# The close of the first routed MLP: norm factors in halves between other operations, five tiles on VectorE, beta added in the MLP

## The chip, the cores and the metric

The program runs on one core of one Trainium2 chip. The metric is its time on the device in microseconds. A core has TensorE (matrix products), VectorE (DVE in the profile), ScalarE (ACT), GpSimd (POOL) and SyncE (SP, here only a queue of DMA issues). Each engine works through its own list of instructions in order; engines meet by semaphores.

## The reference

The program is an audio tower of four layers. 32 sequences of 125 tokens are cut to 87 tokens each, 2784 tokens of width 192, and then pass attention and feed-forward blocks. The change lies in the feed-forward block of layer 0 and in how its result is made ready for layer 1:

```
def _L0_ffn_ref(x, w1, b1, w2, b2, down_w, down_b, up_w, gamma, beta):
    logits = _gelu(x @ w1 + b1) @ w2 + b2
    routing = softmax(logits); sparse = the two largest of 8, scaled to sum 1
    z = _gelu(einsum('bsh,ehd->bsed', x, down_w) + down_b)
    expert_out = einsum('bsed,edh->bseh', z, up_w)
    moe_out = einsum('bseh,bse->bsh', expert_out, sparse)
    return _layer_norm(x + moe_out, gamma, beta)

h = h + _L0_ffn_ref(_layernorm(h), ...)
h = h + _L1_attn_ref(_layernorm(h), ...)     # quantises its input by its largest absolute value
```

## The kernel before

Tokens lie in 22 tiles of 128 (the last has 96), `H` is the residual h and `X` (`l0f_x`) its normalised copy x, both [128, 22, 192] in SBUF. The program is a row of stages; each is a block in which every engine has its own list, and all engines meet at its end. `Kit.stage` also counts semaphores: once more than 100 have been given out, it clears them on GpSimd (L105) and adds a barrier of all engines (L106) ahead of the stage that is opened.

The stages around the change are l0f_router, l0f_dispatch, l0f_mlp (the routed MLP, 51 tiles of 128 routed rows), l0f_tail, l1a_turn, l1a_qkv and so on; l1a_close is stage 19 and l1f_front stage 20.

In l0f_mlp (`routed_mlp_stage`) GpSimd gathers the rows of a tile by an indirect DMA (L852), TensorE turns and expands them, ScalarE applies gelu (L963), TensorE projects, VectorE multiplies by the routing weight (L1005), and GpSimd scatters the result to DRAM (L856). The function has an argument `beside`: an operation that VectorE does behind the multiplication of each of the first 22 tiles. Two later MLPs use it, this one does not.

l0f_tail then closes the block. The tiles go in four parts (`PARTS`: 6, 6, 5 and 5 tiles). SyncE issues ten loads of the routed rows into `back` (L1940). VectorE adds beta to all of `H` (L1964), clears the unused rows of `back` (L1966), and then by parts adds both choices to `X` (L1970) and takes the statistics of each tile (L1972). `find_factors` (L1947 to L1962) makes from them the mean, the variance and 1/std of all 22 tiles at once: six steps, a square root on ScalarE (L2000), seven steps more. Each step is issued by `link`, which waits until the one before has ended. ScalarE applies the factors, one operation a tile (L2004), and reports each part. VectorE follows by parts: times gamma (L1976), plus `H` (L1977), which is the new residual, and its statistics (L1979). The same again for the norm of layer 1: factors of all 22 tiles, ScalarE applies them, VectorE takes the largest absolute value by parts (L1985) and over the parts (L1986), and GpSimd over the partitions (L1991).

The order of the work is the order of these lists; nothing else schedules it.

Of the kernel before, what the change touches and what calls it, by code (L numbers as in the profile page):

```python
# [16 lines left out]
ALU = mybir.AluOpType  # L17
ACT = mybir.ActivationFunctionType
# [11 lines left out]
D = 192  # L30
TP = 128
# [1797 lines left out]
def l0_ffn(kit, H, stats, X1, l1a):  # L1829
    nc, dram = kit.nc, kit.dram  # L1830
    E, R = 8, 96
    with ExitStack() as outer:
# [77 lines left out]
        routed_mlp_stage(kit, "l0f_mlp", route, ex, ACT.Gelu)  # L1910
# [3 lines left out]
PARTS = ((0, 6), (6, 12), (12, 17), (17, 22))  # L1914


def l0f_tail_stage(kit, route, X, H, gb, stats, x_max):
# [5 lines left out]
    R = route.choices  # L1923
    with kit.stage("l0f_tail") as ctx:
# [18 lines left out]
        def _(dve):  # L1943
            link, v = Chain(dve, chain), nc.vector

            def find_factors(u):
                dve.wait_ge(stats_done, (u + 1) * TN)  # L1947
                me, ve, mo, vo = (stats[:, :, k] for k in (1, 2, 4, 5))
                link(v.tensor_tensor(tmp[u][:], me, mo, ALU.subtract))
                link(v.scalar_tensor_tensor(mean[u][:], tmp[u][:], 0.5, mo, ALU.mult, ALU.add))  # L1950
                link(v.scalar_tensor_tensor(tmp[u][:], tmp[u][:], D / 4.0, tmp[u][:], ALU.mult, ALU.mult))
                link(v.tensor_tensor(var[u][:], vo, tmp[u][:], ALU.add))
                link(v.tensor_tensor(var[u][:], var[u][:], ve, ALU.add))
                v.tensor_scalar(var[u][:], var[u][:], 1.0 / D, LN_EPS, ALU.mult, ALU.add).then_inc(var_ready, 1)
# [12 lines left out]
            for q, (a, z) in enumerate(PARTS):  # L1967
# [5 lines left out]
            find_factors(0)  # L1973
            for q, (a, z) in enumerate(PARTS):
                dve.wait_ge(applied, q + 1)
                link(v.tensor_tensor(X[:, a:z, :], X[:, a:z, :], across(gb[:, 0, :], 1, z - a), ALU.mult))  # L1976
                link(v.tensor_tensor(H[:, a:z, :], X[:, a:z, :], H[:, a:z, :], ALU.add))  # L1977
# [1853 lines left out]
```

## Time and profile before

| | us |
|---|---|
| median of 3 runs | 2314.96 |
| lowest and highest run | 2313.03, 2317.95 |
| span of the profiled execution | 2358.7 |
| l0f_tail, first load issued to the last small reduction's start | 697.75 to 756.15 |
| TensorE busy | 1698.8 (72%) |
| VectorE busy | 1290.5 (55%) |
| ScalarE busy | 1022.7 (43%) |
| GpSimd busy | 343.4 (15%) |

The profiled execution's own time is not listed apart from its span, which is from its first instruction to its last. Durations below come from that one execution. Times in the timelines are from the start of its span. An instruction's own duration can overlap that of the next on the same engine; where a row stands for several (x22), its duration is the time that they cover together.

### The profile page before, as it was taken

Reading aid. Unit: us, or ns where it says so; the run is one execution under the profiler, and the core shown is the slowest. Engines: PE = TensorE matmul, PEld = TensorE weight load, DVE = VectorE, ACT = ScalarE, POOL = GpSimd, SP = SyncE. Lnnn points to the kernel's source line nnn. Section 1 sums busy time; section 2 is a strip of 40 time slices with the busy share of each in tenths; the row PEclk is TensorE's granted clock in tenths of the full one; section 3 lists DMA queues with packets and bytes.
Section 4 is the critical chain, followed back from the end, with each engine's and each line's share of the span. In section 5 each row is a group of like instructions: output and inputs, shape, how many; then the busy total and the mean of one; then the engine's idle time right before and its main releaser. Section 6 shows DMA issues by size and latency. Waiting matters only on the chain. (4 is left out here: it accounts for less than half of the span.)

```text
span 2358.7 us, 35978 instructions
## 1 busy us (share of the span) xinstructions
PE 1698.8 (72%) x12150; PEld 1375.5 (58%) x12166; DVE 1290.5 (55%) x2688; ACT 1022.7 (43%) x2115; POOL 343.4 (15%) x415
## 2 busy tenths in 40 slices
PE   3588879856760489966499686664893698469995
PEld 2265657745650355545489563443683598369995
DVE  6588963361137879968622468997316211642223
ACT  4466753312234568865112147873322254312221
POOL 0000000006640000001143100000000342034431
PEclk9799979977885589986699797775996699689998
DMA  3200000214450000000466300000004453446775
GB/s 85 71 18 19 21 23 9 49 50 128 136 164 16 2 7 7 5 1 12 140 214 212 108 4 8 7 4 1 13 1 127 135 179 118 130 139 223 223 218 191
DMA packets 137245, 189.82 MB, mean 80 GB/s; under 512 B 51661, under 2 KB 111213, under 8 KB 137069
## 3 DMA queue, kind: packets, MB, share of 16 engines
q1 hardware_dynamic: 116289, 146.91, 20.3%
q0 software_dynamic: 15360, 36.72, 5.4%
q10 hardware_dynamic: 5420, 3.91, 0.6%
q8 instruction: 103, 1.69, 0.3%
q14 instruction: 73, 0.60, 0.1%
HBM read 150.21 MB, written 33.68 MB: 78 GB/s over the span
## 5 line engine op out<-in xcount | busy, mean ns | idle before, releaser
L989 DVE TENSOR_TENSOR 36_l3f_mlp_hidden<-36_l3f_mlp_gate,36_l3f_mlp_first 128x512 f32<-128x512 f32 x51 | 35.1, 688 | 185.0 <-ACT 36_l3f_mlp_gate L967 101.0
L882 PE MATMUL 36_l3f_mlp_first<-36_l3f_mlp_xT,36_l3f_mlp_w 128*128 128x128 f32 x816 | 101.5, 278 | 1.8 <-issue 1.8
L1245 PE MATMUL 2_performer_p_u<-perf_proj,2_performer_yT 128*87 128x512 f32 (+1 forms) x204 | 94.1, 605 | 10.6 <-DVE 2_performer_arg L1406 9.5
L882 PEld LDWEIGHTS 36_l3f_mlp_first<-36_l3f_mlp_xT,36_l3f_mlp_w 128*128 128x128 f32 x816 | 96.9, 195 | 2.1 <-issue 2.1
L1005 DVE TENSOR_SCALAR 9_l0f_mlp_y<-9_l0f_mlp_second,l0f_routing_weight 128x192 f32<-128x192 f32 x51 | 20.4, 416 | 142.0 <-PE 9_l0f_mlp_second L896 64.4
L967 ACT ACTIVATE 36_l3f_mlp_gate<-36_l3f_mlp_first 128x512 f32<-128x512 f32 x51 | 30.5, 597 | 136.4 <-PE 36_l3f_mlp_first L887 127.4
L1003 DVE TENSOR_TENSOR 32_l3a_mlp_y<-32_l3a_mlp_second,l3a_experts_b_rows 128x192 f32<-128x192 f32 x29 | 10.4, 358 | 136.7 <-issue 106.3
L896 PE MATMUL 36_l3f_mlp_second<-l3f_experts_w,36_l3f_mlp_hidden 128*128 x408 | 81.0, 342 | 0.0
L989 DVE TENSOR_TENSOR 22_l1f_mlp_hidden<-22_l1f_mlp_gate,22_l1f_mlp_first 128x512 f32<-128x512 f32 x29 | 19.9, 687 | 105.8 <-ACT 22_l1f_mlp_gate L967 78.2
L963 ACT ACTIVATE 32_l3a_mlp_hidden<-32_l3a_mlp_first,l3a_experts_b_cols 128x128 f32<-128x128 f32 x174 | 48.1, 377 | 65.5 <-PE 32_l3a_mlp_first L887 47.6
L2618 ACT ACTIVATE l1a_p<-14_pla_f,l1a_recip 128x87 int16<-128x87 f32 x272 | 71.7, 354 | 9.2 <-DVE l1a_recip L2693 9.2
L856 POOL DMA_INDIRECT l3f_results<-36_l3f_mlp_y,l3f_routing_put x51 | 50.2, 984 | 136.2 <-DVE 36_l3f_mlp_y L1005 136.2
L896 PEld LDWEIGHTS 36_l3f_mlp_second<-l3f_experts_w,36_l3f_mlp_hidden 128*128 128x128 f32 x408 | 66.0, 192 | 6.5 <-issue 0.5
L1245 PEld LDWEIGHTS 2_performer_p_u<-perf_proj,2_performer_yT 128*87 128x87 f32 x204 | 33.3, 177 | 60.2 <-issue 57.6
L896 PE MATMUL 32_l3a_mlp_second<-l3a_experts_w,32_l3a_mlp_hidden 128*128 x348 | 66.0, 341 | 2.6 <-ACT 32_l3a_mlp_hidden L963 2.6
L896 PE MATMUL 9_l0f_mlp_second<-l0f_experts_w,9_l0f_mlp_hidden 128*128 x204 | 53.5, 391 | 19.7 <-issue 15.9
L963 ACT ACTIVATE 9_l0f_mlp_hidden<-9_l0f_mlp_first,l0f_experts_b_cols 128x128 f32<-128x128 f32 x102 | 32.0, 363 | 71.9 <-PE 9_l0f_mlp_first L887 44.8
L930 ACT ACT_TABLE_LOAD x4 | 5.1, 1283 | 133.4 <-PEq L605 92.9
L896 PEld LDWEIGHTS 32_l3a_mlp_second<-l3a_experts_w,32_l3a_mlp_hidden 128*128 128x128 f32 x348 | 57.4, 194 | 6.9 <-issue 3.7
L887 PE MATMUL 36_l3f_mlp_first<-36_l3f_mlp_xT,36_l3f_mlp_w 64*128 64x128 f32 x816 | 60.2, 286 | 0.5 <-issue 0.3
L882 PE MATMUL 22_l1f_mlp_first<-22_l1f_mlp_xT,22_l1f_mlp_w 128*128 128x128 f32 x464 | 58.6, 280 | 1.0 <-issue 0.9
L1879 POOL PARTITION_ALL_REDUCE l1a_mx<-6_l0f_hidden_wide x1 | 0.4, 387 | 404.5 <-issue 404.5
(914 smaller groups left out, 4964.0 us busy)
## 6 DMA issues: line engine op xcount, KB each, us to landing
36_l3f_mlp_w<-in_L_ffn_w_dram SPq DMA_DIRECT2D x51, 768.0 KB
22_l1f_mlp_w<-in_L_ffn_w_dram SPq DMA_DIRECT2D x29, 768.0 KB
32_l3a_mlp_w<-in_L_attn_W_dram SPq DMA_DIRECT2D x29, 576.0 KB
9_l0f_mlp_w<-in_L_ffn_down_w_dram SPq DMA_DIRECT2D x51, 192.0 KB
l3a_experts_w<-in_L_attn_W_dram SPq DMA_DIRECT2D x8, 576.0 KB
l1a_blocks<-l1a_qkb SPq DMA_DIRECT2D x192, 5.4 KB, 1.8
l1f_experts_w<-in_L_ffn_w_dram SPq DMA_DIRECT2D x8, 384.0 KB, 6.1
l2a_blocks<-l2a_qkb SPq DMA_DIRECT2D x192, 5.4 KB, 1.8
```

The costliest lines, as they stand in the source:

```text
L856: nc.gpsimd.indirect_dma_start(route.results, to(i), y[i % NY][:], None).then_inc(put[i % NY], 16)
L882: nc.tensor.matmul(to(t + a * PAIRS), of[:, t + a * PAIRS, :], at[:, 0, :], start=(t == 0), stop=True, skip_group_check=True)
L887: ins = nc.tensor.matmul(to(t + a * PAIRS), of[rows, 2 * PAIRS + t, :], at[rows, 1, :], start=False, stop=True, skip_group_check=True)
L896: ins = nc.tensor.matmul(second[j % 2][:, 0:D], hidden[j % 2][:, t, :], ex.w2[:, ds(expert[j], 1), t, :].rearrange("p a w -> p (a w)"), st ...
L930: nc.scalar.preload_act_table(func)
L963: ins = nc.scalar.activation(out[:, t], src[:, t // PAIRS, t % PAIRS, :], func, bias=ex.b1_cols[:, ds(e, 1), t])
L967: nc.scalar.activation(out[:], src[:, 0, 0:HT, :], func).then_inc(done, 1)
L989: v.tensor_tensor(hidden[j % 2][:], gate[j % 2][:], first[j % 2][1][:, 0, 0:HT, :], ALU.mult).then_inc(hidden_done, 1)
L1003: ins = v.tensor_tensor(y[i % NY][:], of, ex.b2_rows[:, ds(e, 1), :].rearrange("p a w -> p (a w)"), ALU.add)
L1005: ins = v.tensor_scalar(y[i % NY][:], of, route.weight[:, i:i + 1], None, ALU.mult)
L1245: ins = t.matmul(p_u[:, k, 0:(EIGHT - h) * M], yT[b % 2][:, k, :], proj[:, h:EIGHT, :].rearrange("p h m -> p (h m)"), start=True, stop=True)
L2618: ins = a(P[:, j, n, :], f[j % 2][:, n * NT:(n + 1) * NT], ACT.Copy, scale=recip[:, j, n:n + 1])
```

## The change

1. Beta goes into the routed MLP: 22 additions of 128 x 192, by `beside` (L1911 of the new kernel), in place of one of 128 x 4224 in the tail. The clearing of `back` goes to GpSimd.
2. The factors are made by halves (`HALF`: tiles 0 to 11 and 12 to 21). `find_factors` becomes a generator: each `next` issues one step, and the next step waits for it before it is issued. The steps of one half stand between the sums, products and statistics of the other half's parts; only the second half's factors of the second norm (and six steps of those of the first) stand in a row.
3. The last part of the second norm, five tiles, is applied by VectorE with `tensor_scalar`, and its maximum is taken first.
4. Three semaphores are added (`factor`, `cleared`, `summed`). With them the clearing in `Kit.stage` falls ahead of l1a_close, before it fell ahead of l1f_front; and one of the later clearings has five ranges where it had four.

```diff
-        routed_mlp_stage(kit, "l0f_mlp", route, ex, ACT.Gelu)
+        routed_mlp_stage(kit, "l0f_mlp", route, ex, ACT.Gelu,
+                         beside=lambda link, v, i: link(v.tensor_tensor(H[:, i, :], H[:, i, :], gb[:, 1, :], ALU.add)))
...
+HALF = ((0, 2), (2, 4))
...
-                link(v.tensor_tensor(tmp[u][:], me, mo, ALU.subtract))
-                link(v.scalar_tensor_tensor(mean[u][:], tmp[u][:], 0.5, mo, ALU.mult, ALU.add))
...
-            link(v.tensor_tensor(H[:], H[:], across(gb[:, 1, :], 1, TN), ALU.add))
-            for r in range(R):
-                link(v.memset(back[r][LAST:TP, TN - 1, :], 0.0))
...
+            def find_factors(u, h):
+                a, z = span(h)
...
+                dve.wait_ge(stats_done, u * TN + z)
+                small(v.tensor_tensor(t, me, mo, ALU.subtract))
+                yield
+                wait_small()
+                small(v.scalar_tensor_tensor(m, t, 0.5, mo, ALU.mult, ALU.add))
+                yield
...
+                v.tensor_scalar(w, w, 1.0 / D, LN_EPS, ALU.mult, ALU.add).then_inc(var_ready, 1)
+                yield
+                dve.wait_ge(std_ready, 2 * u + h + 1)
+                small(v.reciprocal(r, s))
+                yield
...
+            def collect(q, steps):
+                a, z = PARTS[q]
                 dve.wait_ge(loaded[q], 16 * R * (2 if z == TN else 1))
                 for r in range(R):
-                    link(v.tensor_tensor(X[:, a:z, :], X[:, a:z, :], back[r][:, a:z, :], ALU.add))
+                    v.tensor_tensor(X[:, a:z, :], X[:, a:z, :], back[r][:, a:z, :], ALU.add).then_inc(summed, 1)
+                    done["summed"] += 1
+                    some(steps)
+                    dve.wait_ge(summed, done["summed"])
                 for i in range(a, z):
                     v.bn_stats(stats[:, i, :], X[:, i, :]).then_inc(stats_done, 1)
+                    some(steps)
...
+            none = iter(())
+            dve.wait_ge(cleared, R)
+            collect(0, none)
+            collect(1, none)
+            early = find_factors(0, 0)
+            collect(2, early)
+            collect(3, early)
+            whole(early)
+            late = find_factors(0, 1)
+            some(late, 6)
+            close(0, late)
+            whole(late)
+            close(1, none)
+            early = find_factors(1, 0)
+            some(early)
+            close(2, early)
+            close(3, early)
+            whole(early)
+            whole(find_factors(1, 1))
+            dve.wait_ge(factors_ready, 4)
+            a, z = PARTS[MINE]
+            for i in range(a, z):
+                v.tensor_scalar(X[:, i, :], H[:, i, :], rstd[1][:, i:i + 1], less[1][:, i:i + 1], ALU.mult,
+                                ALU.add).then_inc(summed, 1)
+            dve.wait_ge(summed, done["summed"] + z - a)
+            link(v.memset(X[LAST:TP, TN - 1, :], 0.0))
+            largest(MINE)
+            for q in range(MINE):
                 dve.wait_ge(applied, len(PARTS) + q + 1)
...
+            root(0, 0)
+            act.wait_ge(factors_ready, 1)
+            apply(0, 0, X)
+            root(0, 1)
+            apply(0, 1, X)
+            act.wait_ge(factors_ready, 2)
+            apply(0, 2, X)
+            apply(0, 3, X)
+            root(1, 0)
+            act.wait_ge(factors_ready, 3)
+            root(1, 1)
+            apply(1, 0, H)
+            apply(1, 1, H)
+            act.wait_ge(factors_ready, 4)
+            apply(1, 2, H)
```

`close` is `collect` for gamma and the residual: product, a step, sum, a step, and a step behind each tile's statistics. `some` issues one step (or n), `whole` all that are left.

On VectorE, from the sums of the third part on, the list before was this (`l0f_x` is `X`, `10_l0f_tail_back` the routed rows, x5 is five in a row):

```order
L1970 TENSOR_TENSOR l0f_x<-l0f_x,10_l0f_tail_back 128x960 x2
L1972 BN_STATS stats<-l0f_x 128x6 x5
L1970 TENSOR_TENSOR l0f_x<-l0f_x,10_l0f_tail_back 128x960 x2
L1972 BN_STATS stats<-l0f_x 128x6 x5
L1949 TENSOR_TENSOR 10_l0f_tail_tmp<-stats 128x22
L1950 SCALAR_TENSOR_TENSOR 10_l0f_tail_mean<-10_l0f_tail_tmp,stats 128x22
L1951 SCALAR_TENSOR_TENSOR 10_l0f_tail_tmp<-10_l0f_tail_tmp 128x22
L1952 TENSOR_TENSOR 10_l0f_tail_var<-stats,10_l0f_tail_tmp 128x22
L1953 TENSOR_TENSOR 10_l0f_tail_var<-10_l0f_tail_var,stats 128x22
```

and is now this, down to the fourth statistics of that part:

```order
L2014 TENSOR_TENSOR l0f_x<-l0f_x,10_l0f_tail_back 128x960
L1964 TENSOR_TENSOR 10_l0f_tail_tmp<-stats 128x12
L2014 TENSOR_TENSOR l0f_x<-l0f_x,10_l0f_tail_back 128x960
L1967 SCALAR_TENSOR_TENSOR 10_l0f_tail_mean<-10_l0f_tail_tmp,stats 128x12
L2019 BN_STATS stats<-l0f_x 128x6
L1970 SCALAR_TENSOR_TENSOR 10_l0f_tail_tmp<-10_l0f_tail_tmp 128x12
L2019 BN_STATS stats<-l0f_x 128x6
L1973 TENSOR_TENSOR 10_l0f_tail_var<-stats,10_l0f_tail_tmp 128x12
L2019 BN_STATS stats<-l0f_x 128x6
L1976 TENSOR_TENSOR 10_l0f_tail_var<-10_l0f_tail_var,stats 128x12
L2019 BN_STATS stats<-l0f_x 128x6
L1979 TENSOR_SCALAR 10_l0f_tail_var<-10_l0f_tail_var 128x12
```

The steps of the first half's factors have moved up from behind all statistics to behind each of the third and fourth part's operations.

On ScalarE the tail's list before was:

```order
L1997 ACT_TABLE_LOAD
L2000 ACTIVATE 10_l0f_tail_std<-10_l0f_tail_var 128x22
L2004 ACTIVATE l0f_x<-l0f_x,10_l0f_tail_less,10_l0f_tail_rstd 128x192 x22
L2000 ACTIVATE 10_l0f_tail_std<-10_l0f_tail_var 128x22
L2004 ACTIVATE l0f_x<-H,10_l0f_tail_less,10_l0f_tail_rstd 128x192 x22
```

and is now:

```order
L2084 ACT_TABLE_LOAD
L2089 ACTIVATE 10_l0f_tail_std<-10_l0f_tail_var 128x12
L2093 ACTIVATE l0f_x<-l0f_x,10_l0f_tail_less,10_l0f_tail_rstd 128x192 x6
L2089 ACTIVATE 10_l0f_tail_std<-10_l0f_tail_var 128x10
L2093 ACTIVATE l0f_x<-l0f_x,10_l0f_tail_less,10_l0f_tail_rstd 128x192 x16
L2089 ACTIVATE 10_l0f_tail_std<-10_l0f_tail_var 128x12
L2089 ACTIVATE 10_l0f_tail_std<-10_l0f_tail_var 128x10
L2093 ACTIVATE l0f_x<-H,10_l0f_tail_less,10_l0f_tail_rstd 128x192 x17
```

The root is taken four times for a half each, the second one between the first two parts, the last two together ahead of the second norm's tiles, of which ScalarE keeps 17.

## Rows read from the trace of the kernel before

**Rows 1.** Busy times by stretch of l0f_tail: length, busy us of each engine, PEclk.
```profile
core 0: us, PE busy (x) PEld busy (x) DVE busy (x) ACT busy (x) POOL busy (x), PEclk, DMA share, GB/s
...
719.30:725.30 6.00, 0.00 (x0) 0.00 (x0) 2.53 (x14) 3.00 (x8) 0.00 (x0) 0.50 0.00 0
...
741.50:747.50 6.00, 0.00 (x0) 0.00 (x0) 2.53 (x14) 3.00 (x8) 0.00 (x0) 0.50 0.00 0
```

**Rows 2.** Timeline of l0f_tail, first factors: start us, us, engine line op [idle before <-releaser].
```profile
717.87 1.40 DVE L1972 BATCH_NORM_STATS2 stats<-l0f_x 128x6 f32<-128x192 f32 x5
719.30 0.20 DVE L1949 TENSOR_TENSOR 10_l0f_tail_tmp<-stats 128x22 f32<-128x22 f32 x1
...
720.44 0.18 DVE L1954 TENSOR_SCALAR 10_l0f_tail_var<-10_l0f_tail_var 128x22 f32<-128x22 f32 x1
720.65 0.22 ACT L2000 ACTIVATE 10_l0f_tail_std<-10_l0f_tail_var 128x22 f32<-128x22 f32 x1 [21.61 <-DVE 10_l0f_tail_var L1954]
720.90 0.29 DVE L1956 RECIPROCAL 10_l0f_tail_rstd<-10_l0f_tail_std 128x22 f32<-128x22 f32 x1 [0.29 <-ACT 10_l0f_tail_std L2000]
...
722.52 9.75 ACT L2004 ACTIVATE l0f_x<-l0f_x,10_l0f_tail_less,10_l0f_tail_rstd 128x192 f32<-128x192 f32 x22 [1.65 <-DVE 10_l0f_tail_less L1962]
725.29 1.36 DVE L1976 TENSOR_TENSOR l0f_x<-l0f_x,l0f_gb 128x1152 f32<-128x1152 f32 x1 [2.80 <-ACT l0f_x L2004]
```

**Rows 3.** The same timeline, second factors and end of the stage.
```profile
741.49 0.20 DVE L1949 TENSOR_TENSOR 10_l0f_tail_tmp<-stats 128x22 f32<-128x22 f32 x1
...
744.72 9.74 ACT L2004 ACTIVATE l0f_x<-H,10_l0f_tail_less,10_l0f_tail_rstd 128x192 f32<-128x192 f32 x22 [1.66 <-DVE 10_l0f_tail_less L1962]
...
754.96 1.15 DVE L1985 TENSOR_REDUCE 10_l0f_tail_part_max<-l0f_x 128x1 f32<-128x960 f32 x1
756.15 0.16 DVE L1986 TENSOR_REDUCE 10_l0f_tail_row_max<-10_l0f_tail_part_max 128x1 f32<-128x4 f32 x1
```

**Rows 4.** The same timeline, start of the stage.
```profile
697.75 4.92 SPq L1940 DMA_DIRECT2D 10_l0f_tail_back<-l0f_results  x10
...
697.80 4.56 DVE L1964 TENSOR_TENSOR H<-H,l0f_gb 128x4224 f32<-128x4224 f32 x1 [3.18 <-PEq L806]
702.45 0.53 DVE L1966 MEMSET 10_l0f_tail_back<- 32x192 f32 x2
703.10 2.75 DVE L1970 TENSOR_TENSOR l0f_x<-l0f_x,10_l0f_tail_back 128x1152 f32<-128x1152 f32 x2
```

**Rows 5.** Timeline of l3f_out, the last stage, which issues the same loads.
```profile
2337.75 6.06 SPq L1070 DMA_DIRECT2D 37_l3f_out_back<-l3f_results  x10
2343.01 2.75 DVE L1090 TENSOR_TENSOR H<-H,37_l3f_out_back 128x1152 f32<-128x1152 f32 x2 [8.41 <-DMA 37_l3f_out_back<-l3f_results]
...
2346.90 5.14 DVE L1090 TENSOR_TENSOR H<-H,37_l3f_out_back 128x1152 f32<-128x1152 f32 x4 [1.14 <-DMA 37_l3f_out_back<-l3f_results]
```

**Rows 6.** Groups of the routed MLP (busy us, mean ns, idle us); another MLP's addition.
```profile
L856 POOL DMA_INDIRECT l0f_results<-9_l0f_mlp_y,l0f_routing_put x51 | 49.7, 974 | 46.3 <-DVE 9_l0f_mlp_y L1005 34.9 <-issue 11.3
...
L1005 DVE TENSOR_SCALAR 9_l0f_mlp_y<-9_l0f_mlp_second,l0f_routing_weight 128x192 f32<-128x192 f32 x51 | 20.4, 416 | 142.0 <-PE 9_l0f_mlp_second L896 64.4 <-remote 42.8 <-issue 34.8
...
L2266 DVE TENSOR_TENSOR H<-H,l3a_x x22: 348/349/350, 1873.5 to 1969.3; 128x192 f32<-128x192 f32 x22
```

**Rows 7.** Timeline of VectorE in an earlier stage, 12-wide operations, no wait between.
```profile
116.10 0.16 DVE L1435 TENSOR_TENSOR 2_performer_arg<-2_performer_rmax,2_performer_p_top 87x12 f32<-87x12 f32 x1 [5.31 <-PE 2_performer_p_top L1257]
116.19 0.22 DVE L1440 RECIPROCAL 2_performer_rden<-2_performer_p_out 87x12 f32<-87x12 f32 x1
```

**Rows 8.** Timeline of VectorE, 22 tiles normalised with two pointer operands.
```profile
458.84 6.46 DVE L211 TENSOR_SCALAR l0f_x<-H,5_norm_mean,5_norm_rstd 128x192 f32<-128x192 f32 x22
```

**Rows 9.** Gaps ahead of l1a_close and l1f_front; the clearing (ns min/median/max).
```profile
1086.12 0.06 DVE L3072 MEMSET 19_l1a_close_m<- 128x1 f32 x1 [0.60 <-PEq L2718]
...
1115.37 0.20 DVE L1767 TENSOR_TENSOR 20_l1f_front_tmp<-stats 128x22 f32<-128x22 f32 x1 [2.18 <-PEq L106]
...
L105 POOLq DRAIN  x19: 57/88/112, 532.8 to 2052.1; - x19
L105 POOLq EVENT_SEMAPHORE_RANGE_CLEAR  x19: 46/174/243, 532.9 to 2052.5; - x19
```

More of the change, by code:

```diff
@@ L1923, in l0f_tail_stage @@
     R = route.choices
+    MINE = len(PARTS) - 1
     with kit.stage("l0f_tail") as ctx:
@@ L1968, in _, with some, whole @@
+            def some(steps, n=1):
+                for _ in range(n):
+                    next(steps, None)
+            def whole(steps):
+                for _ in steps:
+                    pass
+            def collect(q, steps):
+                a, z = PARTS[q]
                 dve.wait_ge(loaded[q], 16 * R * (2 if z == TN else 1))
                 for r in range(R):
-                    link(v.tensor_tensor(X[:, a:z, :], X[:, a:z, :], back[r][:, a:z, :], ALU.add))
+                    v.tensor_tensor(X[:, a:z, :], X[:, a:z, :], back[r][:, a:z, :], ALU.add).then_inc(summed, 1)
+                    done["summed"] += 1
+                    some(steps)
+                    dve.wait_ge(summed, done["summed"])
@@ L1971, in _, with close @@
                 for i in range(a, z):
                     v.bn_stats(stats[:, i, :], X[:, i, :]).then_inc(stats_done, 1)
-            find_factors(0)
-            for q, (a, z) in enumerate(PARTS):
+                    some(steps)
+            def close(q, steps):
+                a, z = PARTS[q]
                 dve.wait_ge(applied, q + 1)
-                link(v.tensor_tensor(X[:, a:z, :], X[:, a:z, :], across(gb[:, 0, :], 1, z - a), ALU.mult))
-                link(v.tensor_tensor(H[:, a:z, :], X[:, a:z, :], H[:, a:z, :], ALU.add))
+                v.tensor_tensor(X[:, a:z, :], X[:, a:z, :], across(gb[:, 0, :], 1, z - a), ALU.mult).then_inc(summed, 1)
+                done["summed"] += 1
+                some(steps)
+                dve.wait_ge(summed, done["summed"])
+                v.tensor_tensor(H[:, a:z, :], X[:, a:z, :], H[:, a:z, :], ALU.add).then_inc(summed, 1)
+                done["summed"] += 1
+                some(steps)
+                dve.wait_ge(summed, done["summed"])
@@ L1978, in _, with largest @@
                 for i in range(a, z):
                     v.bn_stats(stats[:, i, :], H[:, i, :]).then_inc(stats_done, 1)
-            find_factors(1)
-            for q, (a, z) in enumerate(PARTS):
+                    some(steps)
+            def largest(q):
+                a, z = PARTS[q]
+                link(v.tensor_reduce(part_max[:, q:q + 1], X[:, a:z, :], AX.XY, ALU.max, apply_absolute_value=True))
+            none = iter(())
+            dve.wait_ge(cleared, R)
+            collect(0, none)
@@ L1989, in _ @@
         def _(pool):
+            for r in range(R):
+                nc.gpsimd.memset(back[r][LAST:TP, TN - 1, :], 0.0).then_inc(cleared, 1)
             pool.wait_ge(maxed, 1)
@@ L1997, in _, with root, apply @@
             nc.scalar.preload_act_table(ACT.Sqrt)
[L1998 to L2005 removed]
+            def root(u, h):
+                a, z = span(h)
+                act.wait_ge(var_ready, 2 * u + h + 1)
+                a_(std[u][:, a:z], var[u][:, a:z], ACT.Sqrt).then_inc(std_ready, 1)
+            def apply(u, q, of):
+                for i in range(*PARTS[q]):
+                    ins = a_(X[:, i, :], of[:, i, :], ACT.Identity, bias=less[u][:, i:i + 1], scale=rstd[u][:, i:i + 1])
+                ins.then_inc(applied, 1)
+            root(0, 0)
[13 more added lines that the diff above has]
+            apply(1, 2, H)
 def l1_ffn(kit, H, stats, l2a, l2a_arrived, l2a_loads):
```

70 lines of the change are left out of this document (40 added, 30 removed).

## The prediction

> **What bounds the kernel now.** I read the page first: one core, TensorE the busiest engine over the whole span, so a gain on VectorE counts only where TensorE has nothing to do. I then took the busy times by stretches of the stage that is changed (l0f_tail), the timeline of that stage, the timelines of two other stages for prices, and the groups of the routed MLP ahead of it.
>
> The stage has no TensorE work, and its end sets when the next stage can start. Its path is: loads of the routed rows, VectorE's sums and statistics, 13 small steps for the norm factors, ScalarE's first six tiles, VectorE again, the small steps again, ScalarE again, VectorE's maxima. In the two stretches around the factors VectorE is busy 2.53 of 6.00 us [rows 1]: there the small steps run one by one, and then VectorE waits 2.80 us for ScalarE's first part [rows 2, 3]. The clock column says 0.50 there, so TensorE is at 1.2 GHz before and will be at 1.2 GHz after: it is idle either way.
>
> **Beta (part 1).** The 4.56 us addition and the two memsets (0.53 us) stand ahead of the first sum, which starts at 703.10, 5.35 us after the first load was issued [rows 4]. The last stage of the kernel issues the same loads (two blocks of 128 x 1152 first) with nothing on VectorE ahead, and its first sum starts 2343.01 - 2337.75 = 5.26 us after the issue [rows 5]. So the addition lies almost wholly in the shadow of the loads: with it gone the first sum starts at about 697.75 + 5.26 = 703.0, at best 0.1 us earlier. I take 0.05. What is late next is the load itself. The second part's rows land 9.15 us after the issue by [rows 5], 706.90; VectorE wants them at 707.4, so they stay hidden, by 0.5 us. The memsets go to GpSimd, idle there; they would have to take over 5 us to be seen.
>
> In the routed MLP the addition comes back as 22 pieces of 128 x 192. The same piece in another routed MLP takes 349 ns; with its wait some 0.39 us. VectorE is idle 142 us before its 51 multiplications there, 2.8 us a tile [rows 6], so I take 0. If every piece delayed its tile it would be 22 x 0.39 = 8.6 us; that end is kept.
>
> **Interleaved small steps (part 2).** A step that waits for the one before costs 0.23 us (719.30 to 720.44 for five) [rows 2]. One with no such wait costs less: a 12-wide operation on VectorE starts at 116.10 and the next at 116.19 [rows 7], so 0.09 us at most; I take 0.085. Behind a sum or a product, whose result is waited for anyway, I take 0.025 (0 to 0.05). The reciprocal (290 ns against 180) I take at 0.2. It also needs ScalarE's root: from the last variance step to the reciprocal pass 0.46 us [rows 2], while one statistics operation (0.26, from five in 1.40) and the step itself give 0.35, so a stall of 0.1.
>
> On this the Trainium skill speaks against the change: "VectorE: DVE Perf Modes", section "The DRAIN you can't avoid", says that the next operation does not start until the pipe is empty, with or without semaphores between, and its rules for authors say to reduce the number of operations and not of semaphores. The rows disagree: 0.09 us from start to start [rows 7], while the first operation itself is shown with 0.16 us. By that rule the interleaving would win nothing; it is a rival below.
>
> Now the path, on the clock of the profiled execution:
> - First half's factors. They are hidden in parts 2 and 3 of the collecting. Part 2 grows by 4 x 0.085 + 0.2 + 0.1 + 2 x 0.025 = 0.69, part 3 by 3 x 0.085 = 0.26 up to the place of the last step. This stands ahead of the fifth statistics operation, before at 717.87 + 4 x 0.264 = 718.93; now 718.93 - 0.05 + 0.95 = 719.83. ScalarE starts 0.21 us later, as it did after the last step [rows 2], at 720.04. Before: 722.52. Gain so far 2.5 us, and VectorE's product of part 0 starts at 725.29 - 2.48 = 722.81. In the meantime VectorE finishes collecting (720.3) and does six waited steps of the second half (1.3 us, 721.6): not late.
> - The products, sums and statistics took 725.29 to 741.49, 16.20 us [rows 2, 3]. They take up the rest: part 0 gets seven steps, the reciprocal under a product (5 x 0.085 + 0.05 = 0.48); ahead of part 2 there is one step with a wait for the last statistics (0.2); part 2 gets seven (0.69); part 3 gets five, two of them under a product or a sum (0.31). Sum 1.68, so 722.81 + 17.88 = 740.69. The gain has shrunk to 0.8 us: the interleaving pays back its own steps, since VectorE is full here. ScalarE's parts 1 to 3 keep ahead: part 1 is done at some 725.7, and is wanted at 727.6.
> - Last factors. Only the second half's 13 steps are left in a row. ScalarE no longer waits for them: it waits for the first half (ready) and for the second half's variance, which is six steps in: 740.69 + 1.1 + 0.21 = 742.0, then the root, and its first tile at 742.14. Before: 744.72 [rows 3]. A gain of 2.6 us.
> - Five tiles to VectorE. ScalarE has 17 tiles instead of 22, at 9.75 us for 22 (0.439 each and 0.1 more): done at 742.14 + 7.56 = 749.70. VectorE: factors at 740.69 + 3.2 = 743.9, five tiles at 6.46/22 = 0.29 each [rows 8], 745.4, memset 0.25, maximum of its own part 1.19 (754.96 to 756.15, [rows 3]), 746.9, part 0 to 748.3, part 1 to 749.7. So both engines come to the last maximum together at 749.7, and the small reduction starts at 750.9. Before: 756.15. The stage gains 5.25 us.
>
> **Elsewhere (part 3).** The stage allocates three more semaphores. The helper that clears them once over 100 are used now does so one stage earlier, ahead of l1a_close and no longer ahead of l1f_front. The gap on VectorE is 0.60 us without and 2.18 us with the clearing [rows 9], so some 1.6 us move and nothing is gained: both are barriers of all engines. One further clear is issued later on (20 against 19), a drain and a range clear of 0.09 + 0.17 us [rows 9]: 0.26 us lost.
>
> **Sum.** 5.25 - 0.26 = 5.0 us. The profiled execution has a span of 2358.7 us, so it would come to 2353.7. The runs have 2314.96 as their median, 43.7 us less than that span; the stage has no TensorE work whose clock could explain a part of this, so I carry the 5.0 us over unscaled: 2314.96 - 5.0 = 2310.0 us. A measurement of this kernel can tell about 0.2% (4.6 us) from no change, so the forecast lies right at that bound.
>
> **Rivals.**
> 1. Full price for every small step. If a step behind another operation costs 0.22 instead of 0.085, 22 of them on the path take 22 x 0.135 = 3.0 us back: gain 2.0, 2313.0 us. For it: the rule cited above, and that each step still has a wait instruction ahead of it. Against it: [rows 7].
> 2. Beta really comes off the path. If the loads land soon after 698, the whole 4.56 + 0.53 us goes too, as the diff suggests at first sight: 2310.0 - 5.0 = 2305.0 us. Against it: the 5.26 us with an idle VectorE [rows 5].
> 3. Slower: beta delays the routed MLP. Each piece sits in VectorE's queue ahead of the next tile's multiplication, for which GpSimd's scatter and, two tiles on, TensorE wait. Price up to 0.39 us a piece, 8.6 us, giving 2318.6 us. It decides from 5.0/22 = 0.23 us exposed per piece on: then the kernel is slower than before. For it: of 46.3 us that GpSimd idles ahead of its scatters, 34.9 are put down to VectorE's product. Against it: 2.8 us of idle VectorE a tile [rows 6].
> 4. The clearing, moved, or what comes after the shorter stage, costs or gives a few us in the TensorE stages behind. Nothing in the rows asks for it.
>
> **How the numbers follow.** Forecast 0.62, rival 1 0.12, rival 2 0.06, rival 3 0.10, the rest 0.10. The forecast's own range is 2308 to 2312: small steps wholly hidden would give 1.9 us more, 0.05 us more per step 1.1 us less. The three runs of the kernel before lie between 2313.0 and 2318.0, so about 2 us of spread comes on either side, and rival 1 and a part of rival 3 lie inside: 2305.5 to 2315.5. Faster by over 0.2% (below 2310.3): six tenths of the forecast, rival 2, a third of the rest: 0.47. Slower by over 0.2% needs nearly all of rival 3 or something unseen: 0.09. Within: 0.44.
>
> **What would show it.** The first sum at 5.2 to 5.4 us after the first load issue (step 1; 1 us or less would be rival 2). VectorE start to start of a small step between two statistics 0.08 to 0.09 us (0.22: rival 1). ScalarE's first tile of the first pass some 22.3 us after the issue, of the second some 44.4 us; the last maximum some 52 us after it, with VectorE waiting less than 0.5 us there. The routed MLP as long as before, to 1 us. The gap ahead of l1a_close 1.6 us longer and that ahead of l1f_front 1.6 us shorter. The prediction is wrong if the stage gains under 4 or over 6 us, or if the MLP or a stage behind moves by over 2 us.

## The result and the profile after

The changed kernel took 2310.57 us (median of 20 runs, 2304.79 to 2317.28) against 2315.53 us for the kernel before (20 runs on the same chip, 2311.29 to 2337.33). The ratio is 0.9968 [0.9954, 0.9981], so 4.4 to 10.7 us faster. Measured twice more it was 0.9975 [0.9956, 0.9993] and 0.9973 [0.9954, 0.9992].

The profiled execution of the changed kernel has a span of 2307.4 us. In it the changed stage goes from its first load (669.03) to the start of the small reduction (721.92) in 52.89 us. Before it took 756.15 - 697.75 = 58.40 us [rows 3, 4]. The stage gained 5.51 us; 5.25 were forecast. All times "after the issue" below are counted from that first load, since the stage now starts earlier in the span.

The start of the stage in the timeline of the changed kernel (start, duration, engine line operation, idle time before), which answers to [rows 4]:

```profile
669.03 5.32 SPq L1944 DMA_DIRECT2D 10_l0f_tail_back<-l0f_results  x10
...
674.56 2.75 DVE L2014 TENSOR_TENSOR l0f_x<-l0f_x,10_l0f_tail_back 128x1152 f32<-128x1152 f32 x2 [8.69 <-DMA 10_l0f_tail_back<-l0f_results]
677.35 1.66 DVE L2019 BATCH_NORM_STATS2 stats<-l0f_x 128x6 f32<-128x192 f32 x6
```

With nothing on VectorE ahead of it the first sum still starts only 5.53 us after the issue, and it is the DMA that ends the wait. The two memsets now lie on GpSimd and are over at 669.48.

The same timeline from the last statistics of the collecting to the product of part 0, which answers to [rows 2]:

```profile
691.13 0.15 DVE L2000 SCALAR_TENSOR_TENSOR 10_l0f_tail_less<-10_l0f_tail_mean,10_l0f_tail_rstd 128x12 f32<-128x12 f32 x1
...
691.33 2.73 ACT L2093 ACTIVATE l0f_x<-l0f_x,10_l0f_tail_less,10_l0f_tail_rstd 128x192 f32<-128x192 f32 x6 [3.98 <-DVE 10_l0f_tail_less L2000]
691.59 0.18 DVE L1964 TENSOR_TENSOR 10_l0f_tail_tmp<-stats 128x10 f32<-128x10 f32 x1
...
692.63 0.17 DVE L1979 TENSOR_SCALAR 10_l0f_tail_var<-10_l0f_tail_var 128x10 f32<-128x10 f32 x1
693.97 0.19 ACT L2089 ACTIVATE 10_l0f_tail_std<-10_l0f_tail_var 128x10 f32<-128x10 f32 x1
...
694.09 1.36 DVE L2025 TENSOR_TENSOR l0f_x<-l0f_x,l0f_gb 128x1152 f32<-128x1152 f32 x1 [1.28 <-ACT l0f_x L2093]
```

ScalarE's first tile comes at 691.33, 22.30 us after the issue; before it was 722.52 - 697.75 = 24.77. What VectorE does meanwhile are six waited steps of the second half (each of them waits for the end of the one before), 0.21 us apart. It then waits 1.28 us for ScalarE's six tiles, where it waited 2.80 us.

The same timeline, second factors and end, which answers to [rows 3]:

```profile
711.66 0.18 DVE L1964 TENSOR_TENSOR 10_l0f_tail_tmp<-stats 128x10 f32<-128x10 f32 x1
...
712.70 0.17 DVE L1979 TENSOR_SCALAR 10_l0f_tail_var<-10_l0f_tail_var 128x10 f32<-128x10 f32 x1
712.98 0.21 ACT L2089 ACTIVATE 10_l0f_tail_std<-10_l0f_tail_var 128x10 f32<-128x10 f32 x1 [5.83 <-DVE 10_l0f_tail_var L1979]
713.09 7.54 ACT L2093 ACTIVATE l0f_x<-H,10_l0f_tail_less,10_l0f_tail_rstd 128x192 f32<-128x192 f32 x17
...
714.70 1.54 DVE L2063 TENSOR_SCALAR l0f_x<-H,10_l0f_tail_rstd,10_l0f_tail_less 128x192 f32<-128x192 f32 x5
...
716.59 3.93 DVE L2039 TENSOR_REDUCE 10_l0f_tail_part_max<-l0f_x 128x1 f32<-128x960 f32 x3
720.73 1.15 DVE L2039 TENSOR_REDUCE 10_l0f_tail_part_max<-l0f_x 128x1 f32<-128x960 f32 x1 [0.21 <-ACT l0f_x L2093]
721.92 0.16 DVE L2071 TENSOR_REDUCE 10_l0f_tail_row_max<-10_l0f_tail_part_max 128x1 f32<-128x4 f32 x1
```

ScalarE starts its second pass 0.39 us after the sixth step of the second half, and does not wait for the other seven. It does 17 tiles; VectorE does its own five at 0.30 us each and then the maxima. The last maximum waits 0.21 us for ScalarE: both engines arrive together.

Busy times by stretch around the two sets of factors, answering to [rows 1] (length, PE, PEld, DVE, ACT, POOL busy, PEclk):

```profile
690.60:696.60 6.00, 0.00 (x0) 0.00 (x0) 4.51 (x15) 5.28 (x13) 0.00 (x0) 0.50 0.00 0
711.70:717.70 6.00, 0.00 (x0) 0.00 (x0) 5.11 (x20) 4.72 (x12) 0.00 (x0) 0.50 0.00 0
```

VectorE is busy 4.51 and 5.11 us of 6, where it was 2.53, and ScalarE 5.28 and 4.72 where it was 3.00. The granted clock stays 0.50, that is 1.2 GHz, with TensorE idle, as before.

The interleaved steps themselves, from the last part of the collecting (690.12 to 690.79) and from the third and fourth part of the second pass (706.75 on; VectorE, five pieces of one timeline):

```profile
690.12 0.16 DVE L1991 TENSOR_SCALAR 10_l0f_tail_tmp<-10_l0f_tail_tmp 128x12 f32<-128x12 f32 x1
690.18 0.35 DVE L2019 BATCH_NORM_STATS2 stats<-l0f_x 128x6 f32<-128x192 f32 x1
690.45 0.15 DVE L1994 TENSOR_TENSOR 10_l0f_tail_tmp<-10_l0f_tail_tmp,10_l0f_tail_rstd 128x12 f32<-128x12 f32 x1
...
690.79 0.15 DVE L1997 TENSOR_TENSOR 10_l0f_tail_rstd<-10_l0f_tail_rstd,10_l0f_tail_tmp 128x12 f32<-128x12 f32 x1
...
706.75 0.15 DVE L1979 TENSOR_SCALAR 10_l0f_tail_var<-10_l0f_tail_var 128x12 f32<-128x12 f32 x1
706.82 0.35 DVE L2034 BATCH_NORM_STATS2 stats<-H 128x6 f32<-128x192 f32 x1
...
707.18 0.23 DVE L1982 RECIPROCAL 10_l0f_tail_rstd<-10_l0f_tail_std 128x12 f32<-128x12 f32 x1
...
707.54 0.15 DVE L1985 TENSOR_TENSOR 10_l0f_tail_tmp<-10_l0f_tail_rstd 128x12 f32<-128x12 f32 x1
707.61 1.15 DVE L2025 TENSOR_TENSOR l0f_x<-l0f_x,l0f_gb 128x960 f32<-128x960 f32 x1
708.67 0.17 DVE L1988 TENSOR_TENSOR 10_l0f_tail_tmp<-10_l0f_tail_tmp,10_l0f_tail_var 128x12 f32<-128x12 f32 x1
708.79 1.16 DVE L2029 TENSOR_TENSOR H<-l0f_x,H 128x960 f32<-128x960 f32 x1
```

A step whose result the next operation does not need starts 0.06 to 0.07 us ahead of that operation (707.54 to 707.61), though it is itself shown with 0.15 us. From one step to the next, with a statistics operation of 0.27 us between (690.12, 690.45 and 690.79), it is 0.33 to 0.34 us, so 0.07 for the step. Between two of the 960-wide operations a step costs nothing: they start 1.18 us apart with one (707.61, 708.79), and 1.18 us apart without one in the kernel with the steps in a row (below: 709.27, 710.45).

The routed MLP, groups of the changed kernel that answer to [rows 6], with beta's 22 pieces (busy us, mean ns | idle us ahead):

```profile
L1005 DVE TENSOR_SCALAR 9_l0f_mlp_y<-9_l0f_mlp_second,l0f_routing_weight 128x192 f32<-128x192 f32 x51 | 21.3, 418 | 107.3 <-DMA l0f_results<-9_l0f_mlp_y,l0f_routing_put 78.0 <-PE 9_l0f_mlp_second L896 29.2
...
L1911 DVE TENSOR_TENSOR H<-H,l0f_gb 128x192 f32<-128x192 f32 x22 | 7.7, 349 | 0.0
```

Beta takes 7.7 us of VectorE, and VectorE still idles 107.3 us ahead of its 51 multiplications.

The clearing, answering to [rows 9]:

```profile
1052.36 0.06 DVE L3177 MEMSET 19_l1a_close_m<- 128x1 f32 x1 [2.12 <-PEq L106]
...
1080.02 0.20 DVE L1767 TENSOR_TENSOR 20_l1f_front_tmp<-stats 128x22 f32<-128x22 f32 x1 [0.58 <-PEq L3093]
```

```profile
L105 POOLq DRAIN  x20: 54/78/107, 532.0 to 2007.0; - x20
L105 POOLq EVENT_SEMAPHORE_RANGE_CLEAR  x20: 68/133/243, 532.1 to 2007.1; - x20
```

The gap ahead of l1a_close is 2.12 us (0.60 before) and that ahead of l1f_front 0.58 us (2.18 before). One clear more is issued, 20 and not 19; what it costs on the way to the end no row shows.

### The profile page after: what moved, and what is told of

It reads as the page before. It is cut to its first block and busy times, and to the rows that moved or that the text cites. A ratio compares the mean times of both kernels' runs of the same rounds, so it can differ in the third digit from the quotient of the medians.

```text
span 2307.4 us, 36049 instructions
## 1 busy us (share of the span) xinstructions
PE 1687.5 (73%) x12166; PEld 1356.6 (59%) x12166; DVE 1299.0 (56%) x2738; ACT 1023.1 (44%) x2112; POOL 345.4 (15%) x417
## 5 line engine op out<-in xcount | busy, mean ns | idle before, releaser
L1005 DVE TENSOR_SCALAR 9_l0f_mlp_y<-9_l0f_mlp_second,l0f_routing_weight 128x192 f32<-128x192 f32 x51 | 21.3, 418 | 107.3 <-DMA l0f_results<-9_l0f_mlp_y,l0f_routing_put 78.0
L949 ACT ACTIVATE 36_l3f_mlp_xT<-36_l3f_mlp_turned,36_l3f_mlp_nw 128x128 f32<-128x128 f32 x102 | 31.9, 364 | 65.7 <-PE 36_l3f_mlp_turned L869 51.1
L896 PE MATMUL 9_l0f_mlp_second<-l0f_experts_w,9_l0f_mlp_hidden 128*128 x204 | 48.0, 359 | 15.2 <-DVE 9_l0f_mlp_y L1005 8.2
```

Source lines behind the costliest of these rows:

```text
L896: ins = nc.tensor.matmul(second[j % 2][:, 0:D], hidden[j % 2][:, t, :], ex.w2[:, ds(expert[j], 1), t, :].rearrange("p a w -> p (a w)"), st ...
L949: ins = nc.scalar.activation(xT[j % 2][:, k], turned[j % 2][:, k, 0:ROWS], ACT.Identity, scale=nw[j % NW][:, k:k + 1])
L1005: ins = v.tensor_scalar(y[i % NY][:], of, route.weight[:, i:i + 1], None, ALU.mult)
```

## The experiments

Each kernel was timed against the kernel before, on the same chip as those sent with it. "Stage" is from the first load's issue to the start of the small reduction, in the profiled execution. The first sum starts 5.3 to 5.7 us after the issue, as the loads land. Counted from the sum of the second part's rows, which leaves that out, the stage takes 48.7 us in both executions of the kernel before (707.46 to 756.15 in the first) and 43.0 us in all three of the changed kernel; where it matters, this count is given too.

**The changed kernel again.** No edit.

> The changed kernel once more, beside the kernel before. The closing stage took 58.4 us (first load issued to small reduction) before and 52.9 after, 5.5 us less; if the gain is there alone, the time is 5 to 5.5 us below the kernel before (ratio 0.9978). If the routed MLP ahead of it has become shorter too (it was 28 us shorter in the profile), the ratio is clearly lower, towards 0.988, and the MLP in this profile again takes some 139 us from the end of the dispatch to the first load of the closing stage, not 167.

Measured: 2311.25 us, ratio 0.9975 [0.9956, 0.9993]; stage 52.8 us, first sum 5.5 us after the issue. The stage's length repeats to 0.1 us. What follows: differences of a few tenths of a us in the stage can be read from single profiles, while the whole time can't show them.

**The kernel before again**, for its profile.

> The kernel before once more, one profile. If the length of the first routed MLP (167 us in the first profile of before, 139 in that of the changed kernel) is a matter of the execution and not of the change, it may come near 139 here too, with a span near 2312. If the additions of beta make the MLP faster, it stays at 167.

Measured: 2313.55 us (one run), span 2311.3 us; stage 58.3 us, first sum 5.27 us after the issue. Here the clearest difference is in the routed MLP. Windows over the MLP up to the first load, of the execution that the prediction was made from, of this one and of the changed kernel's:

```profile
531.00:698.00 167.00, 123.69 (x714) 99.11 (x714) 21.68 (x58) 50.47 (x155) 99.17 (x102) 0.85 0.45 131
```

```profile
529.00:667.00 138.00, 109.15 (x715) 86.45 (x714) 22.95 (x59) 50.44 (x155) 99.22 (x102) 0.94 0.54 159
```

```profile
530.00:669.00 139.00, 110.06 (x714) 87.38 (x714) 28.40 (x80) 50.30 (x154) 100.08 (x102) 0.94 0.54 158
```

TensorE is busy 109.15 us in 138.0 us here and 110.06 in 139.0 us in the changed kernel, both at a clock of 0.94. In the execution that the prediction was made from the same stretch took 167.2 us at 0.85, with TensorE busy 123.69 us and the DMA engines 0.45 of the time against 0.54; why it took longer no run shows. So the 51 us between that span and the changed kernel's are no effect of the change: the kernel before, profiled again, has 47.4 us less itself, 29.6 of them in this MLP. Its stage is the same to 0.1 us.

**Beta back in the tail**, the rest changed.

```
-routed_mlp_stage(kit, "l0f_mlp", route, ex, ACT.Gelu, beside=...)
+routed_mlp_stage(kit, "l0f_mlp", route, ex, ACT.Gelu)
...
+            link(v.tensor_tensor(H[:], H[:], across(gb[:, 1, :], 1, TN), ALU.add))
             collect(0, none)
```

> The changed kernel with beta again added in one piece at the head of the closing stage. Shadow theory: the 4.56 us addition lies beside the loads, the first sum starts 5.3 to 5.6 us after the first load's issue as without it, the closing stage takes 52.9 us to 0.2, the time is that of the changed kernel to 0.1%. Rival (the move is worth its 4.6 us): the first sum starts some 9.9 us after the issue or the stage is 4 us longer.

Measured: 2309.14 us, ratio 0.9980 [0.9956, 1.0003], stage 52.7 us. The start of its stage in the timeline:

```profile
664.82 5.12 SPq L1943 DMA_DIRECT2D 10_l0f_tail_back<-l0f_results  x10
...
664.87 4.56 DVE L2041 TENSOR_TENSOR H<-H,l0f_gb 128x4224 f32<-128x4224 f32 x1 [3.18 <-PEq L806]
670.14 2.75 DVE L2013 TENSOR_TENSOR l0f_x<-l0f_x,10_l0f_tail_back 128x1152 f32<-128x1152 f32 x2 [0.71 <-DMA 10_l0f_tail_back<-l0f_results]
```

The addition of 4.56 us is back on VectorE, and yet the first sum starts 5.32 us after the issue, and it has waited 0.71 us for the DMA by then. Moving beta is worth nothing in this stage.

**Beta in the MLP alone**: the kernel before, with the 22 pieces in the MLP and without the addition in the tail (the reverse of the diff above, on the kernel before).

> The kernel before with only beta moved into the routed MLP (the clearing of the two buffers stays on VectorE). Shadow theory: same as before, closing stage 58.4 us to 0.3, ratio 1.000. If the 22 pieces cost anything in the MLP: up to 0.39 us each, 8.6 us, ratio up to 1.0037. If the move is worth the addition: ratio 0.998, closing stage 54 us.

Measured: 2315.92 us, ratio 1.0001 [0.9969, 1.0033]; the MLP 138.4 us up to the first load, against 137.6 and 139.2 us in the executions above; stage 58.3 us. It brings nothing in the tail. In the MLP the 8.6 us are ruled out, but a small cost is not. From the end of the dispatch to the first load, the nine profiles with the pieces show 138.1 to 139.6 us (mean 138.8). Two without them show 137.6 (the kernel before) and 138.3 (beta back in the tail); the first profile, with its 167.2 us, is left out. So a cost of up to 1 us or so is neither shown nor excluded.

**Steps in a row.** The halves stay, but each half's steps are issued together instead of one by one behind other operations.

```
-                    some(steps)
...
-            early = find_factors(0, 0)
-            collect(2, early)
-            collect(3, early)
-            whole(early)
+            whole(find_factors(0, 0))
+            collect(2, none)
+            collect(3, none)
...
-            close(0, late)
+            close(0, none)
...
-            early = find_factors(1, 0)
-            some(early)
-            close(2, early)
-            close(3, early)
-            whole(early)
+            whole(find_factors(1, 0))
+            close(2, none)
+            close(3, none)
```

> The changed kernel with each half's small steps in a row where they begin, none between other operations. Cheap-between theory (a step between two others costs some 0.075 us, in a row 0.21): VectorE has 3.2 us for the first half's factors ahead of the third part, 1.6 us behind part 0 and 3.2 us ahead of part 2 of the second pass, and the closing stage comes to some 57.5 us (52.9 in the changed kernel), the time to that of the kernel before within 1 us. Rival (the pipe empties behind each operation in any case, so that interleaving wins nothing): the stage stays at 52.9 to 53.5 us. Second rival (halves alone bring the gain): 54 to 55 us.

Measured: 2315.35 us, ratio 0.9995 [0.9979, 1.0010]; stage 56.8 us. The first half's steps of the second norm in its timeline:

```profile
706.38 0.18 DVE L1964 TENSOR_TENSOR 10_l0f_tail_tmp<-stats 128x12 f32<-128x12 f32 x1
706.60 0.18 DVE L1967 SCALAR_TENSOR_TENSOR 10_l0f_tail_mean<-10_l0f_tail_tmp,stats 128x12 f32<-128x12 f32 x1
...
709.27 1.15 DVE L2023 TENSOR_TENSOR l0f_x<-l0f_x,l0f_gb 128x960 f32<-128x960 f32 x1
710.45 1.16 DVE L2026 TENSOR_TENSOR H<-l0f_x,H 128x960 f32<-128x960 f32 x1
```

Thirteen steps take 2.89 us here (706.38 to 709.27), 0.21 from start to start, where the changed kernel spends 0.07 on one behind statistics and nothing on one behind a product. The stage grows by 3.9 us (3.8 from the second part's sum on), and most of the time gained is gone. Interleaving is the larger part of the change. The 57.5 us expected were 0.7 too many. The 3.9 us are a net figure: ScalarE gets the first half's factors earlier in the list here, and the 1.28 us that VectorE waits for part 0 in the changed kernel are gone.

**All tiles on ScalarE.** VectorE's five tiles go back to ScalarE, VectorE takes the maxima part by part.

```
-            for i in range(a, z):
-                v.tensor_scalar(X[:, i, :], H[:, i, :], rstd[1][:, i:i + 1], less[1][:, i:i + 1], ALU.mult,
-                                ALU.add).then_inc(summed, 1)
...
             apply(1, 2, H)
+            apply(1, 3, H)
```

> The changed kernel with the last five tiles of the second norm on ScalarE as before. If the end is set by both engines at once as in the sum, ScalarE ends 5 x 0.44 = 2.2 us later, and memset and last maximum follow: the closing stage takes 52.9 + 2.5 = 55.4 us. If VectorE alone set the end, its 1.6 us of tiles would go and the stage would be 51.3 to 52.9 us.

Measured: 2316.14 us, ratio 0.9997 [0.9978, 1.0015]; stage 730.41 - 675.23 = 55.2 us. ScalarE's second pass and the small reduction in its timeline:

```profile
719.08 9.72 ACT L2088 ACTIVATE l0f_x<-H,10_l0f_tail_less,10_l0f_tail_rstd 128x192 f32<-128x192 f32 x22
...
730.41 0.16 DVE L2066 TENSOR_REDUCE 10_l0f_tail_row_max<-10_l0f_tail_part_max 128x1 f32<-128x4 f32 x1
```

22 tiles take 9.72 us, and VectorE, which had its factors by 720.7, waits 0.8 to 1.3 us for each part. The five tiles are worth 2.3 us of the stage (2.5 from the second part's sum on). Together with the 3.9 us of the interleaving that is more than the whole gain, so the two depend on each other; the kernel with halves alone, steps in a row and all tiles on ScalarE, was not run. The ratio shows less gain than the stage (3.1 us would be 0.9987, which its interval holds).

**First loads split.** The first part's rows are fetched and summed in two pieces of three tiles, so that the first sum can start earlier.

```
+    PIECES = ((0, 3), (3, 6)) + PARTS[1:]
...
-            for q, (a, z) in enumerate(PARTS):
+            for q, (a, z) in enumerate(PIECES):
```

> The changed kernel with the first part's loads and sums in two pieces of three tiles. If the loads set the start, 3 tiles of both choices (0.59 MB less at some 410 GB/s) bring the first sum to 3.9 to 4.2 us after the first issue, where it was 5.5; two sums more cost 0.4 us, and the second part's rows, which land some 9.2 us after the issue, make VectorE wait for them: 0.5 to 0.9 us gained, stage 52.0 to 52.4 us. If the start is a fixed cost of a transfer, the first sum stays at 5.3 to 5.5 and the stage is 0.4 us longer.

Measured: 2312.5 us, ratio 0.9991 [0.9967, 1.0015]; stage 53.3 us. A miss: I had expected it shorter. The start of its stage:

```profile
668.43 7.03 SPq L1945 DMA_DIRECT2D 10_l0f_tail_back<-l0f_results  x12
...
672.23 1.55 DVE L2015 TENSOR_TENSOR l0f_x<-l0f_x,10_l0f_tail_back 128x576 f32<-128x576 f32 x2 [6.93 <-DMA 10_l0f_tail_back<-l0f_results]
...
675.72 1.55 DVE L2015 TENSOR_TENSOR l0f_x<-l0f_x,10_l0f_tail_back 128x576 f32<-128x576 f32 x2 [1.02 <-DMA 10_l0f_tail_back<-l0f_results]
...
678.71 2.75 DVE L2015 TENSOR_TENSOR l0f_x<-l0f_x,10_l0f_tail_back 128x1152 f32<-128x1152 f32 x2 [0.52 <-DMA 10_l0f_tail_back<-l0f_results]
```

The first sum does start 3.80 us after the issue, 1.7 us earlier, but VectorE then waits 1.02 us for the second piece and 0.52 us for the next part. The sum of the second part's rows starts 10.28 us after the issue; in the changed kernel it is 678.92 - 669.03 = 9.89. The later loads now end VectorE's waits, in place of the first one. From the second part's sum on the stage takes 42.99 us, as in the changed kernel. The prediction's remark that the second part's rows stay hidden by 0.5 us was the warning: there was no more than that to win.

**Head start for ScalarE.** ScalarE takes the first four tiles of the second norm as soon as the first half's factors are there, ahead of the second half's root. It keeps 19 tiles and VectorE three. VectorE takes the maxima in the order in which ScalarE reports the parts, the shared last part third. Once with the split loads, once without.

```
-            root(1, 1)
-            apply(1, 0, H)
+            tiles(1, 0, AHEAD, H)
+            root(1, 1)
+            tiles(1, AHEAD, PARTS[0][1], H).then_inc(applied, 1)
             apply(1, 1, H)
             act.wait_ge(factors_ready, 4)
+            tiles(1, PARTS[3][0], OWN, H).then_inc(applied, 1)
             apply(1, 2, H)
```

> The former kernel, and ScalarE applies four tiles of the second norm before it waits for the second half's variance; of the last part ScalarE takes two tiles and VectorE three. ScalarE is then 1.8 us ahead; VectorE ends with 3 tiles, memset and four maxima: 0.8 us less at the end than the former kernel, stage 51.2 to 51.6 us, against the kernel before 58.3: ratio 0.997. If VectorE's root comes later through this (ScalarE busy with the four tiles), the gain is below 0.3 us.

> The changed kernel with ScalarE four tiles ahead and VectorE at three tiles, but the loads of the first part whole again. The split cost 0.4 us (stage 53.3 against 52.9), the head start brought 1.5 us (51.8 against 53.3); if the two are independent, the stage takes 51.4 us, 6.9 less than before, ratio 0.997. If the head start only made good what the split had delayed, it stays at 52 us or more.

Measured: with split loads 2305.89 us (7 runs), ratio 0.9955 [0.9938, 0.9972], stage 51.8 us; without 2310.33 us, ratio 0.9984 [0.9955, 1.0013], stage 51.9 us. The end of the stage without split loads:

```profile
718.07 1.86 ACT L2092 ACTIVATE l0f_x<-H,10_l0f_tail_less,10_l0f_tail_rstd 128x192 f32<-128x192 f32 x4 [3.99 <-DVE 10_l0f_tail_less L2000]
...
719.96 6.66 ACT L2092 ACTIVATE l0f_x<-H,10_l0f_tail_less,10_l0f_tail_rstd 128x192 f32<-128x192 f32 x15
...
721.58 0.96 DVE L2063 TENSOR_SCALAR l0f_x<-H,10_l0f_tail_rstd,10_l0f_tail_less 128x192 f32<-128x192 f32 x3
...
728.04 0.16 DVE L2070 TENSOR_REDUCE 10_l0f_tail_row_max<-10_l0f_tail_part_max 128x1 f32<-128x4 f32 x1
```

The four tiles lie in the time of the waited steps, and VectorE does not wait at all any more: its four maxima follow one another up to the small reduction. The stage is 1.0 us shorter than the changed kernel's. Both expectations were missed by a little, 51.2 to 51.6 us with split loads and 51.4 without, and the second falls between its two cases. The count from the second part's sum shows why: it is 42.19 us with split loads and 42.18 without, against 42.99 and 43.00 without the head start. So the head start is worth 0.8 us in both, as first expected, and the rest is when the loads land: with the same split loads the second part's sum starts 10.28 us after the issue in one profile and 9.60 in the other (with waits of 0.29 and 0.63 us ahead of it). That the split costs 0.4 us was read from one profile and does not hold. By the stage these two are the best versions. By the whole time it is not shown: with stages 0.1 us apart their times are 4.4 us apart, the interval of the one without split loads holds 1, and both intervals overlap those of the changed kernel.

**The changed kernel a third time**, in the same set.

> The changed kernel beside the former one on the same chip: stage 52.9 us, ratio 0.9975 to 0.998 against the kernel before; the former kernel should be 1.5 us below it, which the times can hardly tell and the stage's length in the profiles can.

Measured: 2308.18 us against 2315.93, ratio 0.9973 [0.9954, 0.9992]; stage 52.9 us.

## Why the prediction was right, point by point

The forecast was 2310.0 us, and 2310.57 were measured. That the two are so close is partly luck: the interval of the gain is 6 us wide, and the medians of the kernel before, from the three runs that the forecast starts with and from the 20 here, differ by 0.57 us themselves. The stage is the better test. It was forecast at 53.15 us and took 52.89, and two errors of opposite sign meet in it: the first sum came 0.23 us later than the path had it (5.30 after the issue, measured 5.53), and from there on the small steps cost 0.49 us less (47.85 by the sum, 47.36 in the profile). Of the ratio's interval the forecast's 5.0 us of gain are inside, near its lower end. The steps:

- *Beta.* Right, and shown: first sum forecast 5.26 us after the issue (5.30 in the path), measured 5.53, just outside the 5.2 to 5.4 named as a sign. Loads of this kernel land 5.3 to 5.7 us after their issue in the profiles, so this is their spread. Rival 2 (beta off the path) falls with the two kernels that move beta alone: there is nothing to take away while the loads are on the way.
- *Small steps.* Taken at 0.085 us behind statistics, measured 0.07; at 0.025 behind a product, measured 0. The first part of the path came out at 22.29 us after the issue (measured 22.30) and part 0's product at 25.06 (measured 25.06), but only because the late first sum hides the cheaper steps: from the first sum to ScalarE's first tile it is 16.99 us by the sum and 16.77 in the profile. The sum also leaves out the two steps under the sums of part 3 (0.05 by its own price), which cost nothing. The statistics of the second norm end at 42.94 by the sum, at 42.63 in the profile (711.66): the overestimate of the step again, 0.31 us behind part 0's product. Rival 1 (full price) falls with the pitch of 0.34 us and with the row of waited steps, which costs 3.9 us of the stage.
 The stall for the root, taken at 0.1 us, is there: the last variance step starts at 706.75, the reciprocal at 707.18, 0.43 us on, and 0.34 of that is the step and the statistics between.
 The rule that the prediction took from the section "The DRAIN you can't avoid" of the Trainium skill's page "VectorE: DVE Perf Modes" does not hold for these operations: the next one starts 0.07 us after a step that is shown with 0.15 us, and 0.21 us after it if it waits for it. By that rule the interleaving would have brought nothing; it brought 3.9 us. The prediction passed over a sentence of the same section that does agree with these rows: a next operation that is not held starts earlier.
- *Last factors and tiles.* ScalarE's second pass forecast at 44.39 us after the issue, measured 44.06; VectorE's own tiles 46.15, measured 45.67; the last maximum 52.0, measured 51.70; the small reduction 53.15, measured 52.89. The 0.3 us of the steps run through to the end. That the two engines meet was right to 0.21 us.
- *Beta in the MLP.* Taken at 0 with 8.6 us as the bad end. 22 pieces, 7.7 us busy, and the MLP takes 138.1 to 139.6 us with them and 137.6 and 138.3 without. Rival 3 with its 8.6 us falls; a cost of up to 1 us or so stays possible.
- *Clearing.* Ahead of l1a_close 1.5 us more, ahead of l1f_front 1.6 us less, as forecast; the additional clear is 78 + 133 ns by the rows, 0.2 us (0.26 taken), if its whole duration counts.
- *Scaling from a profile to the median.* The profiled execution was 43.7 us longer than the median of the runs, and the 5.0 us were carried over unscaled. That was right, since the excess lay in the routed MLPs, not in this stage.
- *Rival 4.* Nothing behind the stage moved that the change could account for. The one stage that does differ, 19 to 20, differs between two executions of the same kernel (last section).

What stays open: three ratios of the changed kernel (4.4 to 10.7, 1.6 to 10.2 and 1.9 to 10.7 us) lie around 6.5 us; the stage and the clear give 5.3, or 5.5 if counted from the second part's sum. The differences of the medians are 5.0, 4.3 and 7.8 us. Whether there is another us somewhere, or one less through beta in the MLP, can't be told, since the spans of one and the same kernel differ by 5 us (2307.4, 2312.2, 2307.3).

## What to carry to other kernels

Ahead of moving an operation off an engine, look at what ends the next wait: here 4.56 us of work lay wholly under a load, and neither taking it out nor putting it back changed the stage. In this stage a chain of small dependent steps costs 0.21 us each in a row and a third of that behind another operation; split the factors so that the chain of one half runs behind the work on the other, and give the first half to the other engine at once (in the two kernels with the head start that was worth 0.8 us more). Where two engines share the tiles at the end of a stage, set the split so that both arrive at the last common operation together.

## What the runs showed of the hardware

In l1a_close VectorE makes eight casts of the same size, some of them beside two GpSimd operations. Six of the casts take 0.34 to 0.36 us, two take longer. The casts and the GpSimd operations in the changed kernel's first and third profile (ns min/median/max):

```profile
L3175 DVE CAST 19_l1a_close_slot<-19_l1a_close_whole x8: 339/352/2151, 1055.0 to 1072.7; 87x768 bf16<-87x768 int16 x8
L3116 POOL TENSOR_TENSOR H<-H,l1a_qb x2: 2727/3130/3533, 1060.1 to 1063.6; 128x1536 f32<-128x1536 f32 x1, 128x1152 f32<-128x1152 f32 x1
```

```profile
L3175 DVE CAST 19_l1a_close_slot<-19_l1a_close_whole x8: 339/342/3604, 1054.2 to 1073.9; 87x768 bf16<-87x768 int16 x8
L3116 POOL TENSOR_TENSOR H<-H,l1a_qb x2: 2723/3064/3406, 1059.1 to 1062.5; 128x1536 f32<-128x1536 f32 x1, 128x1152 f32<-128x1152 f32 x1
```

The same kernel, the same data: the two long casts took 2.15 and 0.64 us in the one and 3.60 and 1.35 us in the other, and the way from stage 19 to stage 20 27.6 and 29.8 us. So the change of the kernel is not what moves it. In the timelines all four long casts end 0.2 us after one of GpSimd's two operations ends (1063.82, 1066.53, 1062.69 and 1065.40, against 1063.61, 1066.31, 1062.48 and 1065.17). What differs is where GpSimd starts: 0.11 us after the start of the third cast in the first profile, so that the fourth is the long one, and 0.02 us ahead of the third in the other. The Trainium skill's page "SBUF — State Buffer", section "SBUF: two separate sides", describes the port pair that VectorE and GpSimd share as a lock held for a whole instruction; a cast that waits until one of GpSimd's two operations is over would look like this. It fits the rows, but no run here took the GpSimd operation away, so it isn't shown. Some 2 us of this kernel's time thus differ from one profiled execution to another, and gains of that size have to be read from the stage, not from the whole.

The sums behind loads of the same two blocks started 5.3 to 5.7 us after the issue, and those behind loads of half the size after 3.8 us.
